# First row of a recurrent matmul chain: VectorE writes the rounded operand itself, the group variance is summed by two matmuls, and the weight splits are placed elsewhere

## The reference

```python
xs = rows of group_norm(x)                        # 48 rows of [4, 1024, 48]
def step(carry, row):
    new = relu(einsum('oc,ncw->now', Wm, carry) + bias) + row
    return new, new
down = [xs[0]] + scan(step, xs[0], xs[1:])        # 47 steps
up = scan(step, down[-1], down[:-1], reverse=True)   # 47 steps
result = x + stack(up..., down[-1])
```

## Time and profile before

| | us |
|---|---|
| median of 3 runs (1665.19 to 1665.38) | 1665.2 |
| the profiled execution | 1665.07 |
| its span | 1663.2 |
| PE busy | 1546.4 (93%) |
| ACT busy | 1358.2 (82%) |
| DVE busy | 1141.4 (69%) |
| POOL busy | 959.4 (58%) |

### The profile page before, as it was taken

How to read it: one execution, slowest core, us unless ns; L and a number is a source line. 1 busy time by engine, 2 the same in 40 slices (tenths; PEclk the granted TensorE clock), 3 DMA queues, 4 the chain that set the end, 5 groups by cost and what they waited for, 6 DMA issues and landing times.

```text
span 1663.2 us, 23710 instructions
## 1 busy us (share of the span) xinstructions
PE 1546.4 (93%) x6812; PEld 1276.7 (77%) x6812; DVE 1141.4 (69%) x3355; ACT 1358.2 (82%) x4265; POOL 959.4 (58%) x1096
## 2 busy tenths in 40 slices
PE   0039999999999999999999999999999999999998
PEld 0027888888888888888888888888888888888886
DVE  5686766766766666666667667666666666676676
ACT  4558888888888888888888888888888888888887
POOL 0057767667667667667675555555555555555554
PEclk9999999999999999999999999999999999999999
DMA  9963232323223232322001434343343434343211
GB/s 370 401 238 110 81 114 76 115 83 108 94 97 108 83 115 76 115 76 77 1 1 39 171 117 169 134 151 140 145 165 120 170 115 172 121 164 137 92 58 57
DMA packets 49459, 207.06 MB, mean 124 GB/s; under 512 B 4016, under 2 KB 11440, under 8 KB 49328
## 3 DMA queue, kind: packets, MB, share of 16 engines
q1 hardware_dynamic: 49184, 205.54, 34.0%
q10 hardware_dynamic: 144, 0.00, 0.0%
HBM read 136.32 MB, written 69.21 MB: 124 GB/s over the span
## 4 chain that ended last, share of the span: by engine, by line
PE 91%; DMA 5%; DVE 3%; ACT 1%; issue 0%; POOL 0%; SPq 0%; ACTq 0%; DVEq 0%
PE bank L634 30%; PE bank L621 30%; PE bank L628 30%; DMA x_ring<-x_rows 5%; DVE turn L470 1%; DVE turn L556 0%; ACT turn L433 0%; DVE d_ring L532 0%; DVE d_ring L529 0%; ACT turn L424 0%; DVE st_lo L536 0%; DVE d_ring L571 0%; DVE moments L495 0%; ACT xn L393 0%; DVE turn L551 0%
## 5 line engine op out<-in xcount | busy, mean ns | idle before, releaser
L621 PE MATMUL bank<-w_hi,st_hi 128*128 128x512 f32 (+1 forms) x2264 | 881.7, 389 | 0.0
L634 PE MATMUL bank<-w_hi,st_lo 128*128 128x512 f32 (+1 forms) x2264 | 879.9, 389 | 0.3 <-POOL st_lo L349 0.2
L628 PE MATMUL bank<-w_lo,st_hi 128*128 128x512 f32 (+1 forms) x2264 | 880.1, 389 | 0.0
L349 POOL TENSOR_TENSOR st_lo<-d_ring,st_hi 128x256 fp32r<-128x256 f32 x650 | 463.6, 737 | 578.6 <-ACT st_hi L442 578.6
L424 ACT ACTIVATE turn<-turn 32x128 f32<-32x128 f32 x2256 | 696.8, 309 | 65.8 <-DVE turn L551 41.8
L556 DVE STREAM_TRANSPOSE turn<-bank 32x128 f32<-32x128 f32 x2256 | 709.4, 314 | 35.5
L634 PEld LDWEIGHTS bank<-w_hi,st_lo 128*128 128x128 f32 (+1 forms) x2264 | 424.1, 187 | 90.7 <-POOL st_lo L349 1.2
L621 PEld LDWEIGHTS bank<-w_hi,st_hi 128*128 128x128 f32 (+1 forms) x2264 | 424.3, 187 | 89.5 <-issue 0.6
L628 PEld LDWEIGHTS bank<-w_lo,st_hi 128*128 128x128 f32 (+1 forms) x2264 | 424.3, 187 | 89.3 <-issue 0.4
L433 ACT ACTIVATE turn<-turn,bias_sb 128x128 f32<-128x128 f32 (+1 forms) x1132 | 362.3, 390 | 41.7 <-DVE turn L556 2.6
L442 ACT ACTIVATE st_hi<-d_ring 128x256 fp32r<-128x256 f32 x650 | 237.2, 415 | 138.1 <-DVE d_ring L571 138.1
(11 more groups left out here) (45 smaller groups left out, 125.5 us busy)
## 6 DMA issues: line engine op xcount, KB each, us to landing
x_ring<-x_rows SPq DMA_DIRECT2D x82, 768.0 KB, 6.3
out_rows<-x_ring SPq DMA_DIRECT2D x47, 768.0 KB, 4.1
down_rows<-d_ring SPq DMA_DIRECT2D x40, 768.0 KB, 4.1
d_ring<-down_rows SPq DMA_DIRECT2D x40, 768.0 KB, 5.6
x_ring<-x_rows SPq DMA_DIRECT2D x5, 3072.0 KB, 25.7
d_ring<-x_rows SPq DMA_DIRECT2D x4, 3072.0 KB, 25.6
x_ring<-x_rows SPq DMA_DIRECT2D x5, 1536.0 KB, 12.5
d_ring<-w_t SPq DMA_DIRECT2D x16, 256.0 KB, 9.8
```

The source lines that it names most:

```text
L349: final = pool.tensor_tensor(slot(st_lo, at, b * KB, (b + 1) * KB), d_chunk(row_of(i), i % CHUNKS, b * KB, (b + 1) * KB), slot(st_hi, at, ...
L621: return pe.matmul(bank[j % BANKS][0:used(j), :], stationary(st_hi, j, k), w_cols(w_hi, o, k), start=(n == 0), stop=False)
L628: return pe.matmul(bank[j % BANKS][0:used(j), :], stationary(st_hi, j, k), w_cols(w_lo, o, k), start=False, stop=final)
L634: return pe.matmul(bank[j % BANKS][0:used(j), :], stationary(st_lo, j, k), w_cols(w_hi, o, k), start=False, stop=final)
```

## The change

1. In the last group ScalarE sums blocks 3 and 5; VectorE's aggregation goes by another order.
2. The channel variances are multiplied by the averaging matrix by a matmul of their own, into the same bank as that of the squared deviations, which then needs no addition before it.
3. Six dummy matmuls run before the means' matmul (once the statistics of block 6 are done), six after the variances'.
4. GpSimd's splits 8 and 9 wait for `spread_ready`, splits 10 to 15 for the fourth pair of chunk 0.
5. For chunk 0 VectorE centres pairs of blocks into `d_ring` and multiplies each by `gn_rstd` straight into `st_hi`, in the order 4-5, 6-7, 0-1, 2-3. Then it scales `d_ring` by halves and forms `st_lo`. Chunks 1 and 2 go as before.
6. Job 0 waits for the high parts by pairs; job 1 does eight high x high, eight low x high, eight high x low.

```diff
-WARM = 8
-ACT_BLOCKS = ((3, 7),) * LAST + ((1, 5),)
-LAST_MOMENTS = ((), (0, 1), (2, 3), (4,), (6, 5, 7))
+WARM_LOADS = 6
+WARM_SCALE = 6
+ACT_BLOCKS = ((3, 7),) * LAST + ((3, 5),)
+LAST_MOMENTS = ((), (0, 1), (2,), (4, 3), (6, 5, 7))
+FIRST_PAIRS = ((4, 6), (6, 8), (0, 2), (2, 4))
...
# GpSimd
-            for t in range(W_SPLIT):
+            for t in range(W_FRONT):
                 w_split(t)
-            pool.wait_ge(first_row, 2)
+            pool.wait_ge(spread_ready, 1)
+            for t in range(W_FRONT, W_SPLIT):
+                w_split(t)
+            pool.wait_ge(first_hi, len(FIRST_PAIRS))
             for t in range(W_SPLIT, W_TILES):
                 w_split(t)
...
# ScalarE
-            first_split(0, 0, KB, K)
-            first_split(1, 0, 0, KB)
             for t in range(W_ROUNDED, W_ROUNDED + 2):
                 w_round(t)
-            first_split(2, 1, 0, K)
+            first_split(1)
             for t in range(W_ROUNDED + 2, W_TILES):
                 w_round(t)
-            first_split(3, 2, 0, K)
+            first_split(2)
...
# VectorE
-            dve.tensor_tensor(spread[:, :], delta[:, :], delta[:, :], ALU.mult).then_inc(bn_step, 1)
-            dve.wait_ge(bn_step, 3)
-            dve.tensor_tensor(spread[:, :], spread[:, :], moments[:, :, 1], ALU.add).then_inc(spread_ready, 1)
+            dve.tensor_tensor(spread[:, :], delta[:, :], delta[:, :], ALU.mult).then_inc(spread_ready, 1)
...
-            first_normalise(0, 0, KB, K)
-            first_normalise(1, 0, 0, KB)
-            first_split(0, 0, KB, K)
-            first_split(1, 0, 0, KB)
-            first_normalise(2, 1, 0, K)
-            first_split(2, 1, 0, K)
-            first_normalise(3, 2, 0, K)
-            first_split(3, 2, 0, K)
+            for n, (k0, k1) in enumerate(FIRST_PAIRS):
+                first_centre(n, 0, k0, k1)
+                dve.tensor_tensor(by_image(slot(st_hi, 0, k0, k1)), by_image(d_chunk(0, 0, k0, k1)),
+                                  table(gn_rstd, k0, k1), ALU.mult).then_inc(first_hi, 1)
+            dve.wait_ge(first_hi, len(FIRST_PAIRS))
+            for n, (k0, k1) in enumerate(((KB, K), (0, KB))):
+                first_scale(0, k0, k1)
+                dve.wait_ge(first_row, n + 1)
+                first_split(0, k0, k1)
+            for c in range(1, CHUNKS):
+                first_centre(len(FIRST_PAIRS) + c - 1, c, 0, K)
+                first_scale(c, 0, K)
+                dve.wait_ge(first_hi, len(FIRST_PAIRS) + c)
+                first_split(c, 0, K)
...
# TensorE
+            def keep_warm(times):
+                for n in range(times):
+                    pe.matmul(bank[5][:, 0:P], group_avg[:, :], group_avg[:, :], start=True, stop=True)
+
             pe.wait_ge(const_ready, 1)
+            pe.wait_ge(stats_done, stats_count(LAST, K - 1))
+            keep_warm(WARM_LOADS)
             pe.wait_ge(moments_ready, K)
             pe.matmul(bank[6][:, 0:K * NI], group_avg[:, :], moments[:, :, 0],
                       start=True, stop=True).then_inc(mean_summed, 1)
+            pe.matmul(bank[7][:, 0:K * NI], group_avg[:, :], moments[:, :, 1], start=True, stop=False)
             pe.wait_ge(spread_ready, 1)
             pe.matmul(bank[7][:, 0:K * NI], group_avg[:, :], spread[:, :],
-                      start=True, stop=True).then_inc(var_summed, 1)
-
-            for n in range(WARM):
-                pe.matmul(bank[5][:, 0:P], group_avg[:, :], group_avg[:, :], start=True, stop=True)
+                      start=False, stop=True).then_inc(var_summed, 1)
+            keep_warm(WARM_SCALE)
...
             for n in range(K):
                 hi_hi(1, n)
+            for n in range(K):
                 lo_hi(1, n)
```

More of the change, by code:

```diff
@@ L373, in w_round, with first_split @@
                 act.activation(w_cols(w_hi, o, k), w_raw[t], ACT.Copy).then_inc(w_hi_ready, 1)
-            def first_split(n, c, k0, k1):
-                act.wait_ge(first_row, n + 1)
-                act.activation(slot(st_hi, c, k0, k1), d_chunk(0, c, k0, k1), ACT.Copy).then_inc(first_hi, 1)
+            def first_split(c):
+                act.wait_ge(first_row, 2 + c)
+                act.activation(slot(st_hi, c, 0, K), d_chunk(0, c), ACT.Copy).then_inc(first_hi, 1)
             act.wait_ge(const_ready, 1)
@@ L517, in _, with first_centre, first_scale, first_split @@
             dve.tensor_scalar(gn_var[:, :], bank[7][:, 0:K * NI], GN_EPS, None, ALU.add).then_inc(bn_step, 1)
-            dve.wait_ge(bn_step, 5)
+            dve.wait_ge(bn_step, 4)
             dve.tensor_tensor(spread[:, :], gn_root[:, :], gn_root[:, :], ALU.mult).then_inc(bn_step, 1)
-            dve.wait_ge(bn_step, 7)
+            dve.wait_ge(bn_step, 6)
             dve.scalar_tensor_tensor(out=delta[:, :], in0=spread[:, :], scalar=-0.5, in1=gn_var[:, :],
                                      op0=ALU.mult, op1=ALU.mult).then_inc(bn_step, 1)
-            dve.wait_ge(bn_step, 8)
+            dve.wait_ge(bn_step, 7)
             dve.scalar_tensor_tensor(out=gn_rstd[:, :], in0=delta[:, :], scalar=1.5, in1=gn_root[:, :],
                                      op0=ALU.add, op1=ALU.mult).then_inc(gn_ready, 1)
-            def first_normalise(n, c, k0, k1):
+            def first_centre(n, c, k0, k1):
+                dve.tensor_tensor(by_image(d_chunk(0, c, k0, k1)), x_chunk(0, c, k0, k1), table(gn_mean, k0, k1),
+                                  ALU.subtract).then_inc(first_centred, 1)
+                dve.wait_ge(first_centred, n + 1)
+            def first_scale(c, k0, k1):
                 dst = by_image(d_chunk(0, c, k0, k1))
-                dve.tensor_tensor(dst, x_chunk(0, c, k0, k1), table(gn_mean, k0, k1), ALU.subtract
-                                  ).then_inc(first_centred, 1)
-                dve.wait_ge(first_centred, n + 1)
                 dve.tensor_tensor(dst, dst, table(gn_rstd, k0, k1), ALU.mult).then_inc(first_row, 1)
-            def first_split(n, c, k0, k1):
-                dve.wait_ge(first_hi, n + 1)
+            def first_split(c, k0, k1):
                 dve.tensor_tensor(slot(st_lo, c, k0, k1), d_chunk(0, c, k0, k1),
@@ L597, in _, with wait_hi, wait_lo @@
                       start=True, stop=True).then_inc(mean_summed, 1)
+            pe.matmul(bank[7][:, 0:K * NI], group_avg[:, :], moments[:, :, 1], start=True, stop=False)
             pe.wait_ge(spread_ready, 1)
             pe.matmul(bank[7][:, 0:K * NI], group_avg[:, :], spread[:, :],
-                      start=True, stop=True).then_inc(var_summed, 1)
-            for n in range(WARM):
-                pe.matmul(bank[5][:, 0:P], group_avg[:, :], group_avg[:, :], start=True, stop=True)
[L605 to L610, removed]
+                      start=False, stop=True).then_inc(var_summed, 1)
+            keep_warm(WARM_SCALE)
+            def wait_hi(j, n):
+                if j == 0:
+                    if n % 2 == 0:
+                        pe.wait_ge(first_hi, 1 + n // 2)
+                elif j < CHUNKS:
                     if n == 0:
-                        pe.wait_ge(ready, first_done(j - CHUNKS))
+                        pe.wait_ge(first_hi, len(FIRST_PAIRS) + j)
+                elif j < STEPS:
+                    if n == 0:
+                        pe.wait_ge(hi_ready, first_done(j - CHUNKS))
                     elif n == KB:
-                        pe.wait_ge(ready, second_done(j - CHUNKS))
+                        pe.wait_ge(hi_ready, second_done(j - CHUNKS))
+            def wait_lo(j, n):
+                if j == 0:
+                    if n in (0, KB):
+                        pe.wait_ge(first_lo, 1 + n // KB)
+                elif j < CHUNKS:
+                    if n == 0:
+                        pe.wait_ge(first_lo, 2 + j)
+                elif j < STEPS:
+                    if n == 0:
+                        pe.wait_ge(lo_ready, first_done(j - CHUNKS))
+                    elif n == KB:
+                        pe.wait_ge(lo_ready, second_done(j - CHUNKS))
             def hi_hi(j, n):
                 o, k = j % 2, KB * blocks_of(j)[n // KB] + n % KB
-                wait_split(hi_ready, first_hi, j, n)
+                wait_hi(j, n)
                 if j < 2:
@@ L632, in lo_hi @@
                 o, k = j % 2, KB * blocks_of(j)[n // KB] + n % KB
-                wait_split(lo_ready, first_lo, j, n)
+                wait_lo(j, n)
                 return pe.matmul(bank[j % BANKS][0:used(j), :], stationary(st_lo, j, k), w_cols(w_hi, o, k),
```

## The result

The changed kernel takes 1668.23 us (median of 17 runs, 1667.67 to 1668.94) against 1665.22 (17 runs, 1665.00 to 1665.44): 3.0 us slower, ratio 1.0018, 95% interval 1.0011 to 1.0024. The forecast was 1668.0. The span of its profiled execution is 1666.2 (before 1663.2).

A forecast was written before the change was run, and what follows sets the result against it. Bound: TensorE's stream and the first row's chain (VectorE, ScalarE, GpSimd), level from 114.9 to 153 us. Steps (a) to (f) delay the first turn 2.83: 1665.07 becomes 1667.9, plus 0.13 for the median, 1668.0; range 1665.4 to 1669.2.

The forecast's parts named there:

- (a): Other statistics blocks, last load of x: gain 0.15 us, between nothing (piece 3 lands no earlier) and 0.27.
- (b): Group constants: the addition goes, its matmul hidden beside delta and square, gain 0.22 us.
- (c): Late splits 8 and 9 hold VectorE's 32-column product of the root: its end comes 0.92 us later.
- rival 1: Tiny two-input VectorE ops aren't held by splits: +2.1 us, 1667.3, chance 0.13.
- (d): Row 0's chunk 0 in four pairs: eight VectorE ops take 2.19 us by the trace rows' price, 1.67 by the skill's.
- (e): Rest of chunk 0, then chunk 1: VectorE takes turns with GpSimd's splits, job 1 begins at 123.8, +2.25 us.
- (f): Chunk 2, held by splits and normalising: first turn at 129.40 instead of 126.57, +2.83 us.
- Rival 4: TensorE's stand after job 0 drops it to 1.2 GHz: +1 to +2 us, 1669.5, chance 0.08.
- Rivals 2 and 3: VectorE and GpSimd run side by side: -2.3 us, 1662.9 (0.13); VectorE gets two ops per turn: 1666.3 (0.10).

The follow-up runs named there:

- run 4: The changed kernel with splits 10 to 15 left out and GpSimd's first normalising ops waiting for chunk 2's low part: 1662.88 us.
- run 7: The kernel before the change, with VectorE's centring and scaling of row 0 reading mean and 1/std from PSUM: 1662.91 us, ratio 0.9988.
- Run 8: The whole change, with VectorE reading mean and 1/std from PSUM in row 0: 1663.86 us.
- 2: The changed kernel with GpSimd's splits 8 and 9 early again, where they were before the change: 1667.17 us.
- run 6: The kernel before with parts 1 to 3 of the change, and splits 8 and 9 waiting for spread_ready: 1665.98 us.
- 5: The kernel before with parts 1 to 3 of the change alone: 1665.04 us beside 1665.27.
- 9: The whole change with mean and 1/std read from PSUM, and splits 8 and 9 early as before the change: 1663.00 us.
- run 3: The changed kernel with dummy matmuls of 128 columns filling TensorE's two stands (idle times), around job 0's end: 1668.16 us.
- run 12: run 11 with longer warm-ups, twelve dummy matmuls ahead of the means and seven after the variances: 1662.15 us.
- 10: The kernel before with parts 1 to 3 of the change, and mean and 1/std read from PSUM: 1662.92 us.
- run 11: Kernel of 9 with splits 10 to 15 re-timed, the Newton step using PSUM inputs, and ScalarE rounding four weight tiles before chunk 1: 1662.34 us, ratio 0.9982.

## Why the prediction was right

The mechanism is shown: VectorE's elementwise ops on two SBUF tensors and GpSimd's ops take turns, and the change put more of the former beside the latter. Taking GpSimd away (run 4) or one SBUF input away (7, 8) gives the time back. By steps:

(a) was off: nothing gained instead of 0.15; the deviation of the means started at 110.36 against 110.34. Statistics of piece 2 did begin early, at 101.38 and not at the forecast 101.65, but VectorE was then ready for piece 3 of the last load 0.45 us before it landed at 104.20, so the bound "nothing" held.

(b) 110.77 against 110.98 for the end of what TensorE waits for: -0.21, as forecast (-0.22).

(c) 0.93 in the profile (1.12 - 0.19), 1.06, 0.94 and 0.86 in three pairs of runs (2 against the changed kernel, 6 against 5, 9 against 8); forecast 0.92. Each pair alone is within the interval of a comparison (about 1.5 us each way); that all three agree, with the profile too, carries it. The Trainium skill (GPSIMD Engine Reference, Key points) names VectorE ops with two SBUF inputs, beside those in a 2-port mode, as the ones that contend with GpSimd, and says nothing of size; the 1.12 us of a 32-column op bear it out, and rival 1 is gone. The shapes with one input in PSUM agree from the other side (0.67 and 0.69 us, run 7).

(d) 2.20 for the eight ops (113.89 to 116.09), forecast 2.19; a 128-column op took 0.29, forecast 0.285. TensorE's first matmul came at 114.56, forecast 114.35. The Trainium skill (Vector Engine (DVE) Microarchitecture Reference, Measured stream behaviour on trn2) gives by its figures about 0.21 per op, an estimate, after overlap in the queue. The trace agrees where an op waits for nothing (114.21 to 114.42), but a scaling waits for its centring and starts 0.32 after it (113.89 to 114.21). Four of the eight wait, so the rows' price was the right one.

(e) The ends at 116.54, 117.98, 119.42, 120.82, 122.52 and 123.24 lie 0.16 to 0.21 behind the forecast ones, most of it the 0.15 of step (a). TensorE began job 1 at 123.96, forecast 123.8.

(f) The first turn could begin at 129.49, forecast 129.40.

Rival 4 came true as an event: the clock fell in job 1, which cost TensorE 1.63 us. It was priced as if it added to the rest, at +1 to +2 with only half hidden. All of it was hidden: TensorE's 4.04 became 3.36 and then 2.92 as its later waits for the first row vanished, and run 3 took the fall away for 0.07 us. That the forecast still met the time so closely is partly luck. It had TensorE wait 0.58 for the first row in job 3, on top of the 0.66 there before; in the profile these waits are gone and the slow job stands in their place. The room behind the first row was 2.92 - 2.41 = 0.51, plus 0.68 and 0.44 of older waits: 1.63, just what the fall took. A longer fall would have added to the time. Rivals 2 and 3 are out by the strict turns from 116 to 122.

## What to carry to other kernels

Before moving elementwise work onto VectorE, look at what GpSimd does at that moment: each VectorE op with two SBUF inputs may wait for a whole GpSimd op, however small it is, so many short ops cost more than few long ones. Putting one of the two inputs (a table, a constant) in PSUM freed the op here; delaying GpSimd's work helps only if its next work is held back too. And a loss on one of two level streams says nothing of its worth until the other is moved away.

## What the runs showed of the hardware

TensorE's two clock levels can be told from the starts of its 512-column matmuls. Where the windows view gives a granted clock of 0.50 (run 6, 117 to 119; run 12, 112 to 115) they are 0.43 apart; in the steady stretch at 1.00 they are 0.227 apart. In the prologue of the other profiles the view doesn't show the level: for the kernel before it gives 1.00 from 111 to 118, and the starts from 115.47 to 117.18 are 0.43 apart all the same. There the distance of the starts is the sign to go by.

By that sign, once the first row is out of the way, the clock in the first matmuls of job 0 goes with the differences between runs of one kernel. The profiled executions of runs 7 and 9 have starts of 0.23 almost from the first, and both are the fastest of theirs (1662.40 of 1662.40 to 1664.29, 1662.37 of 1662.37 to 1663.49). Those of runs 4, 10 and 11 start 0.43 apart up to about 117.3 and lie at the upper end (1663.69 of 1661.94 to 1663.92, 1663.61 of 1661.87 to 1663.67, 1663.47 of 1661.39 to 1663.47). Run 12, with two such starts, is at its median. Run 8 doesn't fit: it has few slow starts and is near its highest, with a stand of 0.58 us before job 1. The kernel before, where the first row covers the clock, stays within 1665.01 to 1665.65 beside run 11. There is one profile of each run, so the link is inferred. The clock touches the constants as well: in the profiles of runs 6, 9 and 12 VectorE waited 0.50 us for the matmul of the means and 0.79 for the root, in those of runs 5, 8 and 11 about 0.73 and 1.01.
